# A gated-delta attention layer in TensorE products of 32 tokens: inverse kept 32 columns wide, joined by DMA, with new orders on all engines

## What is computed

```python
q = _short_conv(h @ wq, conv_q); k = ...; v = ...      # 4 taps, then silu
g = -jnp.exp(A_log)[:, None] * jax.nn.softplus(h @ f_a @ f_b + dt_bias)
beta = jax.nn.sigmoid(h @ b_w)
def step(St, inp):                                     # St: 128 x 128 for each head
    qt, kt, vt, gt, bt = inp
    St = St * jnp.exp(gt)[..., None]
    err = jnp.einsum('bhk,bhkv->bhv', kt, St)
    St = St + bt[..., None, None] * kt[..., None] * (vt - err)[..., None, :]
    ot = jnp.einsum('bhk,bhkv->bhv', qt, St)
    return (St, ot)
```

## Time and profile before

| | us |
|---|---|
| median of 3 runs | 10081.21 |
| lowest and highest | 10078.3, 10083.53 |
| profiled execution, its own time | 10076.55 |
| its span from the first to the last instruction | 10074.8 |
| busy in the span: PE (TensorE's matmuls) | 9255.1 |
| PEld (TensorE's weight loads, beside PE) | 6248.6 |
| DVE (VectorE) | 7405.1 |
| ACT (ScalarE) | 6824.4 |
| POOL (GpSimd) | 3650.0 |

### The profile page before, as it was taken

One profiled execution on the slowest core, in us unless ns is written; L12 is line 12 of the kernel. 1 busy time (PEld: TensorE's weight loads), 2 busy tenths in 40 slices (PEclk: granted clock), 3 DMA queues, 4 the chain that ended last, 5 costly groups with the idle time before them and its releaser, 6 DMA issues. The chain is left out here.

```text
span 10074.8 us, 353404 instructions
## 1 busy us (share of the span) xinstructions
PE 9255.1 (92%) x128948; PEld 6248.6 (62%) x128948; DVE 7405.1 (74%) x13320; ACT 6824.4 (68%) x15797; POOL 3650.0 (36%) x5963
## 2 busy tenths in 40 slices
PE   4799999999999999999999999999999999997888
PEld 2566666666666666666666666666666666663333
DVE  2688878888788878787888878788888787872111
...
GB/s 29 51 38 35 38 35 38 36 37 38 35 38 36 38 36 36 37 37 35 39 35 39 36 36 37 35 39 35 37 36 38 35 37 37 37 37 31 8 8 12
DMA packets 513946, 350.47 MB, mean 35 GB/s; under 512 B 63136, under 2 KB 510752, under 8 KB 512816
## 3 DMA queue, kind: packets, MB, share of 16 engines
q1 hardware_dynamic: 511760, 328.31, 12.3%
...
...
## 5 line engine op out<-in xcount | busy, mean ns | idle before, releaser
L1176 POOL TENSOR_TENSOR KB<-KB,tot 128x256 f32<-128x256 f32 x1290 | 1058.0, 820 | 4010.1 <-PE bank L603 4010.1
L1244 DVE SCALAR_TENSOR_TENSOR acc<-bank,hp,acc 128x510 f32<-128x510 f32 (+2 forms) x2331 | 1714.1, 744 | 81.2 <-ACT hnew L872 17.9
L554 PE MATMUL bank<-hn,w_qkv 128*128 (+1 forms) x3108 | 1535.7, 617 | 1.8 <-issue 1.5
L1351 DVE TENSOR_TENSOR invT<-invT,bank 64x128 f32<-64x128 f32 x2576 | 739.8, 287 | 548.8 <-PE bank L647 531.3
L1306 DVE COPY_PREDICATED BIG<-masks,bank 128x512 f32<-128x512 int32 x1032 | 1040.2, 1008 | 75.0 <-DVE BIG L1306 65.6
L889 ACT ACTIVATE Zm<-bank 64x128 f32<-64x128 f32 x2576 | 707.4, 275 | 518.0 <-PE bank L630 503.2
L630 PEld LDWEIGHTS bank<-invE,BIG 64*64 64x64 f32 x20624 | 702.3, 134 | 498.1 <-issue 436.0
L655 PE MATMUL bank<-ident,invT 128*128 128x128 f32 x5152 | 798.4, 278 | 181.3 <-DVE invT L1351 181.3
L655 PEld LDWEIGHTS bank<-ident,invT 128*128 128x128 f32 x5152 | 592.0, 142 | 536.0 <-DVE BIG L1306 380.4
L647 PEld LDWEIGHTS bank<-invT,Zm 64*64 64x64 f32 x20608 | 706.9, 135 | 329.5 <-issue 286.9
L1318 DVE TENSOR_TENSOR QKF<-QKF,tot 128x512 f32<-128x512 f32 x1289 | 889.3, 690 | 0.6 <-PE bank L603 0.6
...
## 6 DMA issues: line engine op xcount, KB each, us to landing
bb<-beta_rows SPq DMA_DIRECT2D x520, 128.0 KB, 4.0
states<-StC SPq DMA_DIRECT2D x288, 128.0 KB, 1.9
w_qkv<-in_L_attn_wk_dram SPq DMA_DIRECT2D x260, 128.0 KB, 2.2
w_qkv<-in_L_attn_wq_dram SPq DMA_DIRECT2D x260, 128.0 KB, 2.2
w_qkv<-in_L_attn_wv_dram SPq DMA_DIRECT2D x260, 128.0 KB, 2.1
StA<-states SPq DMA_DIRECT2D x259, 128.0 KB, 2.0
w_o<-in_L_attn_wo_dram SPq DMA_DIRECT2D x257, 128.0 KB, 2.0
w_fb<-in_L_attn_f_b_dram SPq DMA_DIRECT2D x260, 64.0 KB, 2.8
```

Source lines behind the costliest of these rows:

```text
L554: mm = eng.matmul(rows(BK["proj_" + "qkv"[n_]]), w_qkv[:, n_, k, :], hn_v[:, k, :, cols], start=(k == 0), stop=(k == KD - 1))
L1176: eng.tensor_tensor(e_, e_, t_.to_broadcast([P, C, P // (2 * m), m]), ALU.mult).then_inc(ev[f"kb_mul{s}"], 1)
L1244: eng.scalar_tensor_tensor(dst, rows(bk)[:, :, 0:BLK - sh], hp[par][:, w_:w_ + 1], dst, ALU.mult, ALU.add).then_inc(ev[("tap_" if t_ < 2 e ...
L1351: x_ = eng.tensor_tensor(o_, o_, ps[rw, :, h * QUART:(h + 1) * QUART].rearrange("p c (n m) -> p c n m", m=1 << s), ALU.subtract)
```

## The change

Blocks of 32 tokens are kept by themselves. For the levels 0 to 4 the matrix, the inverse and its transpose have 32 columns for each chain (`BC`, `inv`), and the 128 partitions hold four blocks of 32 x 32 each. `z_product` and `y_product` run on 32 x 32 tiles, and the turn is an instruction of VectorE (`turn`), which transposes each 32 x 32 block. Level 5 and level 6 no longer make one matrix by a mask: their products are laid out so that each lands where it is used. `x5_product` and `y5_product` join two blocks of 32 to one of 64, `x6_product` and `y6_product` two of 64 to 128. The full matrices `F` (outputs in plane 0, inverse in plane 1) and the lower 64 of the turned inverse (`inv64`) are put together by nine DMAs a step, issued from SP (`spread`, `spread_inverse`); x6, y6, solve and outputs wait for them. The flushes are gone. The products of v with the identity in `residual` are transposes. The scaling of the key by its norm moves from VectorE to GpSimd, the last growth of the keys from ScalarE to GpSimd, that of the queries from ScalarE to VectorE. The masks shrink to 32 rows and columns and are loaded by sixteen DMAs. All `step` functions are written anew, with heads up to i + 6 in work and six steps before the loop, and the banks are dealt out anew.

```diff
-BIG = sb(mid, "BIG", [P, LEVELS + 2, C, P])
-qkT = [BIG[:, 0, :, :], BIG[:, LEVELS + 1, :, :]]
-Am = [BIG[:, 1 + s, :, :] for s in range(LEVELS)]
-Zm = [None] + [tile4(f"Zm{s}") for s in range(1, LEVELS)]
-invT = [tile4(f"invT{i}") for i in range(2)]
-invE0 = sb(mid, "invE0", [P, C, HALF])
-invE = sb(mid, "invE", [P, C, HALF])
+QC, IC, L5, Y5, AC = 0, 1, 2, 3, 4
+BC = [sb(mid, f"BC{i}", [P, AC + LEVELS - 2, C, QUART]) for i in range(2)]
+F = [sb(mid, f"F{i}", [P, 2, C, P]) for i in range(2)]
+inv = [sb(mid, f"inv{i}", [P, C, QUART]) for i in range(2)]
+Zc = [None] + [sb(mid, f"Zc{s}", [P, C, QUART]) for s in range(1, LEVELS - 2)]
+X5 = sb(mid, "X5", [P, C, QUART])
+A6, X6, inv64 = (sb(mid, n_, [P, C, HALF]) for n_ in ("A6", "X6", "inv64"))
...
+        def spread(hi, j, pj):
+            eng.wait_ge(ev["y5_cp"], done(j))
+            eng.wait_ge(ev["inv_m4"], done(j))
+            eng.wait_ge(ev["lvl_e4"], done(j))
+            eng.wait_ge(ev["lvl_e5"], done(j))
+            eng.sem_inc(waited, 1)
+            eng.wait_ge(ev["O_mm"], free(j, 2))
+            eng.sem_inc(waited, 1)
+            lo, up = rows_of(2 * hi), rows_of(2 * hi + 1)
+            for rw, cols, first in ((lo, lo, QC), (up, up, QC), (lo, up, L5)):
+                eng.dma_start(F[pj][rw, :, :, cols].rearrange("p f c n -> p (f c) n"),
+                              BC[pj][rw, first:first + 2, :, :].rearrange("p f c n -> p (f c) n")).then_inc(spread_hi if hi else spread_lo, 16)
+
+        def spread_inverse(j, pj):
+            eng.wait_ge(ev["inv_t4"], done(j))
+            eng.wait_ge(ev["y5_cp"], done(j))
+            eng.sem_inc(waited, 1)
+            eng.wait_ge(ev["y_mm6"], free(j))
+            eng.sem_inc(waited, 1)
+            lo, up = rows_of(0), rows_of(1)
+            for rw, cols, src in ((lo, lo, inv[pj]), (up, up, inv[pj]), (up, lo, BC[pj][:, Y5, :, :])):
+                eng.dma_start(inv64[rw, :, cols], src[rw, :, :]).then_inc(inv64_in, 16)
...
+        def level6(j, pj):
+            eng.wait_ge(ev["kb_mul5"], done(j))
+            eng.wait_ge(ev["qk_up5"], done(j))
+            eng.sem_inc(waited, 1)
+            for ch in range(C):
+                out_ = ps_of("lvl6")[:, ch * HALF:(ch + 1) * HALF]
+                for r in range(2):
+                    rw, up = (slice((x + r) * QUART, (x + r + 1) * QUART) for x in (0, 2))
+                    eng.matmul(out_[rw, :], KB[:, ch, rw], QKF[pj][:, 0, ch, HALF:], start=True, stop=True)
+                    mm = eng.matmul(out_[up, :], QKF[pj][:, 1, ch, up], KB[:, ch, 0:HALF], start=True, stop=True)
+            mm.then_inc(ev["lvl_mm6"], 1)
+        def z_product(s, j, pj):
+            eng.wait_ge(ev[f"lvl_e{s}"], done(j))
+            eng.wait_ge(ev[f"inv_t{s - 1}"], done(j))
+            eng.sem_inc(waited, 1)
+            for ch in range(C):
+                for r in range(4):
+                    rw = slice(r * QUART, (r + 1) * QUART)
+                    mm = eng.matmul(ps_of(f"z{s}")[rw, ch * QUART // 2:(ch + 1) * QUART // 2], BC[pj][rw, AC + s, ch, :],
+                                    inv[pj][rw, ch, :].rearrange("p (n two m) -> p n two m", two=2, m=1 << s)[:, :, 0, :],
+                                    start=True, stop=True)
             mm.then_inc(ev[f"z_mm{s}"], 1)
...
-        def turn(s, tile, par):
...
-                mm = eng.transpose(chains(BK[f"t{s}"])[:, ch, :], invT[par][:, ch, :], ident[:, :])
-            mm.then_inc(ev[f"t_tr{s}"], 1)
...
+        def y5_product(j, pj):
+            eng.wait_ge(ev["z_cp5"], done(j))
+            eng.wait_ge(ev["inv_t4"], done(j))
+            eng.sem_inc(waited, 1)
+            lo, md, hi = (slice(r * QUART, (r + 1) * QUART) for r in range(3))
+            for ch in range(C):
+                out_ = ps_of("y5")[:, ch * QUART:(ch + 1) * QUART]
+                eng.matmul(out_[lo, :], inv[pj][lo, ch, :], X5[lo, ch, :], start=True, stop=True)
+                eng.matmul(out_[md, :], X5[lo, ch, :], inv[pj][lo, ch, :], start=True, stop=True)
+                mm = eng.matmul(out_[hi, :], inv[pj][hi, ch, :], X5[hi, ch, :], start=True, stop=True)
+            mm.then_inc(ev["y_mm5"], 1)
+
+        def x6_product(j, pj):
+            eng.wait_ge(ev["lvl_e6"], done(j))
+            eng.wait_ge(spread_hi, 48 * done(j))
+            eng.sem_inc(waited, 1)
+            for ch in range(C):
+                mm = eng.matmul(ps_of("z6")[0:HALF, ch * HALF:(ch + 1) * HALF], A6[HALF:, ch, :], F[pj][HALF:, 1, ch, HALF:], start=True, stop=True)
+            mm.then_inc(ev["z_mm6"], 1)
+
+        def y6_product(j):
+            eng.wait_ge(ev["z_cp6"], done(j))
+            eng.wait_ge(inv64_in, 48 * done(j))
+            eng.sem_inc(waited, 1)
+            for ch in range(C):
+                mm = eng.matmul(ps_of("y6")[0:HALF, ch * HALF:(ch + 1) * HALF], inv64[0:HALF, ch, :], X6[0:HALF, ch, :], start=True, stop=True)
+            mm.then_inc(ev["y_mm6"], 1)
...
-                eng.matmul(half(BK[f"R{s_}"], 0)[:, b, :], vs[par][:, ch, :], ident[:, :], start=True, stop=False)
-                mm = eng.matmul(half(BK[f"R{s_}"], 0)[:, b, :], QKF[par][:, 1 - par, ch, :], St[:, b, :], start=False, stop=True)
+                eng.matmul(half(f"R{s_}")[:, b, :], vs[par][:, ch, :], ident[:, :], start=True, stop=False, is_transpose=True)
+                mm = eng.matmul(half(f"R{s_}")[:, b, :], QKF[par][:, 1, ch, :], St[:, b, :], start=False, stop=True)
...
+        def take_y6(j, pj):
+            eng.wait_ge(ev["y_mm6"], done(j))
+            eng.wait_ge(ev["W_mm1"], free(j, 2))
+            eng.activation(F[pj][0:HALF, 1, :, HALF:], ps_of("y6")[0:HALF, 0:C * HALF].rearrange("p (c n) -> p c n", c=C),
+                           ACT.Copy, scale=-1.0).then_inc(ev["inv_m6"], 1)
...
-        def round_start(j, pj):
-            eng.wait_ge(ev["qk_raw"], done(j))
-            eng.tensor_scalar(QKF[pj][:, :, :, :], QKF[pj][:, :, :, :], ROUND, -ROUND, ALU.add, ALU.add).then_inc(ev["qk_init"], 1)
+            eng.tensor_tensor(QKF[pj][:, :, :, :].rearrange("p f c n -> p f (c n)"), qk[:, :, :, :].rearrange("p f c n -> p f (c n)"),
+                              a[:, :, :].rearrange("p c n -> p (c n)").unsqueeze(1).to_broadcast([P, 2, C * P]), ALU.mult).then_inc(ev["qk_init"], 1)
...
+        def turn(s, j, pj):
+            eng.wait_ge(ev[f"inv_m{s}"], done(j))
+            if s == 0:
+                eng.wait_ge(inv64_in, 48 * free(j, 2))
+                eng.wait_ge(ev["y_mm5"], free(j, 2))
+            eng.transpose(inv[pj][:, :, :], BC[pj][:, IC, :, :]).then_inc(ev[f"inv_t{s}"], 1)
+
+        def grow_inverse(s, j, pj):
+            eng.wait_ge(ev[f"y_mm{s}"], done(j))
+            eng.wait_ge(ev[f"inv_m{s - 1}"], done(j))
+            o_ = odds(BC[pj][:, IC, :, :], s)
+            eng.tensor_tensor(o_, o_, ps_of(f"y{s}")[:, 0:C * QUART // 2].rearrange("p (n m) -> p n m", m=1 << s),
+                              ALU.subtract).then_inc(ev[f"inv_m{s}"], 1)
```

942 lines of the change are left out of this document (443 added, 499 removed).

## The result

The changed kernel takes **9,663.3 us** (median of 4 executions, 9,654.89 to 9,711.84) against 10,082.1 beside it. The ratio of the mean times is 0.9595, 95% interval 0.9567 to 0.9622. It is faster by 4%, where 14.6% was forecast; the forecast's 8,610 us and its range, 8,250 to 9,150, both miss. The profiled execution, from which all rows of the changed kernel are, took 9,711.84 us and is the slowest of the four, 0.5% over the median.

What follows compares the result with a forecast made beforehand. TensorE was taken to set each of 256 steps of 33.36 us; work of 26.2 plus a wait of 1.35 made 27.5, so 10,076.6 - 1,500 + 35 (extra steps and mask loads) = 8,610 us, range 8,250 to 9,150.

Steps and rivals of the forecast that it cites:

- TensorE's work: TensorE's groups in one step, waits left out: 26.2 us after the change, 24.1 to 33.2 at the terms' ends.
- the last rival: Small tiles on TensorE stand in line, about 0.037 us a record: 10,340 us, slower; chance 0.05.
- The wait behind the table load: TensorE's y1 waits about 1.35 us every step for z1's copy, which ScalarE makes after a table load.
- The transfers: Nine more DMAs a step from SP, landing in about 2.2 us, hidden before x6, y6 and solve 0.
- the margin of 0.6 at solve 0: After y5 ends, the lower half arrives at 6.6 us and TensorE reaches solve 0 at 7.2.
- Rival 2: Hand-overs bind: DMAs landing in 5.3 us make x6, y6 and solve 0 late; 9,226 us (8,920 to 9,500); chance 0.20.
- The clock: TensorE's granted clock inside blocks: 0.99 before, no loss from a lower clock charged in any case.
- a clock below 0.95: Sign of a wrong forecast: inside a block, each microsecond of TensorE's work at 1.2 GHz costs one more.
- The sum: Step of 26.2 + 1.35 = 27.5 us, 5.86 less, over 256 steps, plus 35 us: 8,610 us.

Runs made afterwards that it cites:

- early: Changed kernel with six of the nine transfers of a step issued before y5 and only three after it: 9,255 us, ratio 0.918 to the kernel before.
- clean2: Changed kernel with six of nine transfers issued before y5, ScalarE's table loads behind the copies of z1, U and z3, w_o's load before the state's store: 8,745 us.
- clean2_t32: As clean2, but TensorE's program holds the 32 steps of a block written out, where it held 16 and ran them twice: 8,710 us.

## Why the prediction was wrong

**TensorE's work: right.** The prediction had 31.94 us of work before (33.36 less 1.42) and 26.2 after, a gain of 5.74. The table has 32.0 and 26.3, a gain of 5.7. The terms hold singly: 0.37 to 0.39 us for a small group, 0.37 for x5, 0.60 for y6. That settles the last rival, in which the tiles stand in line: 32 records in 0.37 us are 12 ns a record, and it would have taken 37. The prediction set a rule of the Trainium skill against its rows (TensorEngine Tiling (Array Packing), Restrictions and Gotchas, PSUM pressure): different row tiles cannot access one PSUM bank at the same time. It does not show here: in these groups four row tiles write one bank, each its own 32 partitions of it, and the measurement decides.

**The wait behind the table load: right in kind, hidden.** 1.35 us was forecast before y1, and early shows 1.27 there once the transfers are out of the way. In the changed kernel it was 0.39 on average, because in most steps the transfers held TensorE first.

**The transfers: the step that failed first.** The prediction said "They are hidden, with 0.6 to 0.9 us to spare". It took the issue of one at 0.49 us from the load of bw_s, two of them before the third, eight before the ninth, back to back. In the changed kernel an issue takes 0.60 and the next begins 0.77 behind it, SP's waits and counts included. So the ninth begins 6.13 us behind the first, not 4, and the margin of 0.6 at solve 0 becomes a wait of 1.3. The landing was not the fault: in the step shown the last issue, 0.60 long, ended at 3011.31, so it began at 3010.71, and solve 0 started 2.28 us later; the prediction had 2.2. A smaller part is the start: the first issue began 0.25 us behind the end of y5's copy, where the sum has it begin at once. Rival 2 had the place but not the cause, as it asked for a landing of 5.3. The Trainium skill has the case (Perfetto Trace Analysis, What "DMA-bound" means): a kernel can be bound by the sequencer that issues, which then shows one DMA slice behind the other. SP's rows above agree for the 7.2 us from 3004.15 to 3011.31.

**The clock: the step that was missing.** The prediction kept 0.99 in the blocks; it listed a clock below 0.95 as something that would prove it wrong, "and none of the cases has that". The clock was 0.92. So its term of nothing failed: the runs show 5.25 us of half clock a step, and that it goes with waits at this place. The rows before gave little warning: there TensorE waited 1.66 us a step, and the clock of the earlier trace rows was 0.99. The change put 1.9 us more of waiting into the step, most of it into the very stretch that it also filled with small tiles. The same page of the Trainium skill says under Matmul Optimizations that TensorE scales its power with its use, so that matmuls should come back to back in batches. The runs show the clock and not the power, and there they agree: 0.92 with 3.5 us of idle time a step, 0.98 in clean2 with 1.5. They add that the place of the wait counts.

**The sum again.** Per step, from the table: work −5.7; idle +1.86, where the prediction had −0.07; half clock (5.25 − 0.68) / 2 = +2.3, where it had none. That is −1.59 in place of −5.86; the shortfall of 4.27, times 256, is 1,093 us. The profiled execution, from which these steps are, missed by 1,102 and the median by 1,053. A little under half of the miss is waiting, the rest the clock that came with the waiting. With the transfers issued in time and the table loads out of the way, clean2 runs in 8,745 and clean2_t32 in 8,710 us, the fastest kernel here: 9.9% under the changed one, 1.2% over the forecast.

What stays open: why the level groups wait for "issue", and the 0.26 us a step that level 4 waits for GpSimd's scaling of the keys.
